# Ternary FFN: the last butterfly of the second Hadamard turn on VectorE and GpSimd; the channel attention as a loop, its first loads, and constant products in the last stage

## The reference, cut to what matters

```python
x = x + channel_attention(layernorm(x), ctx, ctx)      # 32 heads of 16 channels, scores 512 x 512
x = x + ternary_ffn(layernorm(x), w_up, w_down)
x = x + causal_attention(layernorm(x), ctx, ctx)       # 16 heads of 32 channels
x = x + workspace_ffn(layernorm(x), ...)               # two rounds, 16 slots

def hbitlinear(x, w, bits):                            # used twice in ternary_ffn
    xh = fwht(x)                                       # Walsh-Hadamard over the last axis, / sqrt(n)
    xq = act_quant(xh, bits)                           # per token: round(x * 127 / absmax)
    return xq @ weight_quant(w).T                      # weights -1, 0, 1 times a scale

h = hbitlinear(x, w_up, 8)                             # 512 -> 1024
out = hbitlinear(square(relu(h)), w_down, 8)           # 1024 -> 512
```

## Time and profile before

| | us |
|---|---|
| runs (3) | 3765.82, 3773.39, 3771.95; median 3771.95 |
| profiled execution | 3779.81 |
| its span in the profile | 3777.9 |
| busy PE, DVE, ACT, POOL | 3537.5, 2887.7, 2554.2, 1741.6 |

### The profile page before, as it was taken

The page is one execution under the profiler, slowest core; times in us unless marked ns, Lnnn a source line. Parts: engine busy times, 40 slices in busy tenths (PEclk is TensorE's granted clock), DMA queues, the critical chain, the costliest instruction groups (busy, mean ns, idle before and its releaser), DMA issues. The chain is left out here.

```text
span 3777.9 us, 73028 instructions
## 1 busy us (share of the span) xinstructions
PE 3537.5 (94%) x25219; PEld 1778.8 (47%) x25219; DVE 2887.7 (76%) x4445; ACT 2554.2 (68%) x6417; POOL 1741.6 (46%) x2148
## 2 busy tenths in 40 slices
PE   6999999999999999889999979999997999999997
PEld 1222222222222222278788855555554666666664
DVE  7888888888888888768878858888886466574745
ACT  3777777777777777667777758878875454545454
POOL 5444444444444444077666624554553233342524
PEclk9999999999999999989999989999999999999999
DMA  7777677676677777433333313333452022120402
GB/s 123 123 124 124 120 122 123 118 123 121 120 124 124 124 124 138 125 99 124 116 118 115 117 61 101 108 107 103 129 177 86 1 68 68 41 95 4 132 1 79
DMA packets 344317, 392.11 MB, mean 104 GB/s; under 512 B 58640, under 2 KB 223120, under 8 KB 343952
## 3 DMA queue, kind: packets, MB, share of 16 engines
q1 hardware_dynamic: 316464, 352.03, 42.0%
q10 hardware_dynamic: 27488, 35.41, 3.7%
HBM read 200.65 MB, written 84.93 MB: 76 GB/s over the span
## 5 line engine op out<-in xcount | busy, mean ns | idle before, releaser
L385 DVE TENSOR_REDUCE a_neg_max<-a_max_ps 128x2 f32<-128x1024 f32 x1024 | 1209.9, 1220 | 199.6 <-PE a_max_ps L497 189.9
L529 ACT ACTIVATE a_P<-a_ring_ps 128x512 f32<-128x512 f32 x2048 | 1085.4, 603 | 407.7 <-PE a_ring_ps L477 398.5
L497 PE MATMUL a_max_ps<-a_K,a_Q 96*128 96x512 bf16 x2048 | 621.3, 385 | 32.6 <-DMA a_Q<-a_q_split 24.6
L477 PE MATMUL a_ring_ps<-a_Q,a_K 98*128 98x512 bf16 x2048 | 627.6, 384 | 14.4 <-DMA a_Q<-a_max_rows 10.1
L514 PE MATMUL a_pv_ps<-a_P,a_V 128*32 128x512 f32 x4096 | 545.7, 605 | 1.8 <-ACT a_out_sb L534 1.8
L477 PEld LDWEIGHTS a_ring_ps<-a_Q,a_K 98*128 98x128 bf16 x2048 | 157.9, 96 | 681.4 <-ACT a_P L529 497.8
L1334 ACT ACTIVATE c_P<-c_s_ps,c_bias 128x128 f32<-128x128 f32 x1024 | 368.1, 384 | 65.1 <-DVE c_bias L1170 64.8
L324 POOL TENSOR_SCALAR a_var_eps<-a_mean_var 128x1 f32<-128x1 f32 x64 | 12.3, 192 | 765.1 <-DVE a_mean_var L401 765.1
L497 PEld LDWEIGHTS a_max_ps<-a_K,a_Q 96*128 96x128 bf16 x2048 | 188.9, 98 | 220.8 <-DMA a_Q<-a_q_split 24.6
L1165 DVE TENSOR_REDUCE c_neg_max<-c_s_ps 128x4 f32<-128x512 f32 x256 | 175.7, 686 | 81.5 <-PE c_s_ps L1260 75.0
L1334 ACT ACTIVATION_READ_ACCUMULATOR c_P<-c_s_ps,c_bias 128x1 f32 x1024 | 228.4, 223 | 0.0
(11 more groups left out here) (271 smaller groups left out, 7267.7 us busy)
## 6 DMA issues: line engine op xcount, KB each, us to landing
a_K<-a_k_split SPq DMA_DIRECT2D x384, 128.0 KB, 7.1
a_Q<-a_q_split SPq DMA_DIRECT2D x378, 128.0 KB, 4.6
heads_out<-a_out_sb ACTq DMA_DIRECT2D x128, 256.0 KB, 4.6
w_first_in<-in_x_dram SPq DMA_DIRECT2D x112, 256.0 KB, 3.6
w_second_in<-in_ctx_dram SPq DMA_DIRECT2D x64, 256.0 KB, 4.9
w_third_in<-in_ctxT_dram SPq DMA_DIRECT2D x64, 256.0 KB, 5.0
x<-b_x SPq DMA_DIRECT2D x64, 256.0 KB, 2.1
c_x_in<-x SPq DMA_DIRECT2D x64, 256.0 KB, 3.6
```

The lines of the kernel that those rows point to most:

```text
L385: dve.tensor_reduce(neg_max[:, p, 2 * u:2 * u + 2], max_ps[u % 2][:, :, :], AX.X, ALU.max, negate=True).then_inc(max_taken, 1)
L477: pe.matmul(ring(s, use_of(k))[:, :], K[i][:, h, n:n + 128], Q[i][:, h, :], start=True, stop=True).then_inc(scores_filled, 1)
L497: last = pe.matmul(max_ps[u % 2][:, j, :], Q[i][0:KROW, h, m:m + 128], K[i][0:KROW, h, :], start=True, stop=True)
L529: act.activation(P[p][k // NT][:, k % NT, :], ring(s, use_of(k))[:, :], ACT.Exp, scale=SCALE).then_inc(exp_done, 1)
```

## The change

In the channel attention `run_steps` keeps the first and last steps unrolled and runs those between in a loop of six steps a turn: 20 turns on TensorE and ScalarE, 19 on SyncE, GpSimd and VectorE. GpSimd makes the first batch's V two steps earlier, and SyncE issues the parts of batch 1 ahead of the inputs of batch 3.

```diff
-def run_steps(eng, first, last, body):
-
-    for k in range(first, last + 1):
+def run_steps(eng, first, loop_from, loop_to, last, body):
+
+    assert (loop_to - loop_from) % 6 == 0
+    for k in range(first, loop_from):
         body(Step(0, k))
+    with eng.Fori(0, (loop_to - loop_from) // 6) as turn:
+        for k in range(6):
+            body(Step(turn, loop_from + k))
+    for k in range(loop_to, last + 1):
+        body(Step(0, k))
...
+                if s.k == -2:
+                    transfer_parts(s)
+                load_rows(s)
...
+                if s.k != -2:
+                    transfer_parts(s)
+            run_steps(sp, -8, 2, 116, 126, step)
...
+                if s.half(3) == 0 and s.exists(3) and s.k != -3:
+                    split_values(s.batch(3), s.slot(3), s.lap(3))
+                if s.k == -5:
+                    split_values(0, 0, 0)
+            run_steps(pool, -6, 4, 118, 126, step)
...
+            run_steps(dve, -7, 1, 115, 125, step)
...
+            run_steps(pe, -2, 2, 122, 128, step)
...
+            run_steps(act, -1, 4, 124, 129, step)
```

```diff
@@ pool: the order of a step
+                if t.k == 0:
+                    scale_heads(0)
+                if t.exists(5):
+                    b, i = t.batch(5), t.slot(5, 2)
+                    pool.wait_ge(uc_done, b + 1)
+                    at_least(pool, t2_filled, b - 1)
+                    v = uc[:, :].rearrange("p (a o d) -> p a o d", a=2, o=2)
+                    w = u[i][:, 4:IK, :].rearrange("p (a o) d -> p a o d", o=2)
+                    pool.tensor_tensor(w[:, :, 1], v[:, :, 0], v[:, :, 1], ALU.subtract).then_inc(u_low_done, 1)
                 if t.exists(2):
...
                     pool.tensor_tensor(x1[:, j, :], x_in[i][:, :], scaled[:, :], ALU.add).then_inc(x1_done, 1)
+                if t.exists(-1):
+                    scale_heads(t.batch(-1))
+                if t.exists(1):
+                    b, j = t.batch(1), t.slot(1, 8)
+                    pool.wait_ge(moments_done, b + 1)
...
@@ vector
-                    dve.tensor_tensor(u[i][:, h:IK].rearrange("p k d -> p (k d)"), ua[:, 0:I // 2], ua[:, I // 2:I], ALU.subtract).then_inc(u_done, 1)
+                    at_least(dve, u_low_done, b)
+                    dve.tensor_tensor(uc[:, :], ua[:, 0:I // 2], ua[:, I // 2:I], ALU.subtract).then_inc(uc_done, 1)
                 if t.exists(1):
...
+                if t.exists(3):
+                    b, i = t.batch(3), t.slot(3, 2)
+                    dve.wait_ge(uc_done, b + 1)
...
+                    dve.tensor_tensor(w[:, :, 0], v[:, :, 0], v[:, :, 1], ALU.add).then_inc(u_done, 1)
@@ tensor
-                    pe.wait_ge(u_done, b * 2 + 2)
+                    pe.wait_ge(u_done, b * 2 + 1)
                     at_least(pe, rnd2_done, b)
-                    for k in range(0, IK, 2):
+                    for k in range(0, IK // 2, 2):
                         pe.matmul(t2_ps[:, k * 128:(k + 2) * 128], u[i][:, k, :], had[:, 0:256], start=True, stop=False)
...
+                    pe.wait_ge(u_done, b * 2 + 2)
+                    pe.wait_ge(u_low_done, b + 1)
+                    for k in range(IK // 2, IK):
+                        last = pe.matmul(t2_ps[:, k * 128:(k + 1) * 128], u[i][:, k, :], had[:, 0:128], start=True, stop=True)
```

```diff
+def keep_busy(pe, bank, tile, n):
+
+    for _ in range(n):
+        pe.matmul(bank, tile[:, :], tile[:, :].unsqueeze(1).to_broadcast([128, 4, 128]), start=True, stop=True)
...
+                    if f.k == 0:
+                        keep_busy(pe, xb_ps[1][:, :], w.spare, 11)
```

More of the change, by code:

```diff
@@ L247, in load_weights, with load_rows, transfer_parts @@
                 sp.dma_start(w_in[:, c, :].rearrange("p (k n) -> p k n", k=src.shape[1]), src).then_inc(w_loaded[c], 16)
+            def load_rows(s):
+                if s.half(8) == 0 and s.exists(8):
+                    b, i = s.batch(8), s.slot(8)
+                    at_least(held, q_split_done, b - (NB - 1))
+                    at_least(held, k_split_done, b - (NB - 1))
+                    at_least(held, v_done, b - (NB - 1))
+                    sp.dma_start(x_in[i][:, :], by_channel(x[b])).then_inc(x_loaded[i], 16)
+                    sp.dma_start(c_in[i][:, :], by_channel(ctx[b])).then_inc(c_loaded[i], 16)
+                    sp.dma_start(cT_in[i][:, :].rearrange("p (t c) -> p t c", t=NT), ctxT[b].rearrange("(t p) c -> p t c", p=128)).then_inc(cT_loaded[i], 16)
+            def transfer_parts(s):
+                if s.half(4) == 0 and s.exists(4):
+                    b, i = s.batch(4), s.slot(4)
+                    if s.k != -4:
+                        held.wait_ge(q_split_done, b + 1)
+                    held.wait_ge(k_split_done, b + 1)
+                    at_least(held, scores_filled, (b - (NB - 1)) * (2 * SCORES))
+                    if s.k != -4:
+                        for n, part in enumerate((0, 0, 1, 1, 0, 2)):
+                            sp.dma_start(Q[i][n * D:(n + 1) * D, :, :], q_split[:, i, part, :]).then_inc(Q_loaded[i], 16)
+                    for n, part in enumerate((0, 1, 0, 1, 2, 0)):
+                        sp.dma_start(K[i][n * D:(n + 1) * D, :, :], k_split[:, i, part, :]).then_inc(K_loaded[i], 16)
             def step(s):
@@ L361, in step @@
                         pool.wait_ge(preset, 2 + 2 * i)
-                if s.half(3) == 0 and s.exists(3):
-                    b, i = s.batch(3), s.slot(3)
-                    held.wait_ge(cT_loaded[i], s.lap(3) * 16 + 16)
-                    at_least(held, pv_done, (b - (NB - 1)) * (2 * NT))
-                    pool.tensor_scalar(V[i][:, :, :, 0:D], cT_in[i][:, :].rearrange("p (t h d) -> p t h d", t=NT, d=D), 1.0, 0.0,
-                                       ALU.mult, ALU.add).then_inc(v_done, 1)
-            run_steps(pool, -6, 126, step)
+                if s.half(3) == 0 and s.exists(3) and s.k != -3:
[3 more added lines that the diff above has]
+            run_steps(pool, -6, 4, 118, 126, step)
             pool.memset(w_half[:, :], 0.5).then_inc(preset, 1)
@@ new lines, in scale_heads @@
+            def scale_heads(b):
+                i = b % 4
+                pool.wait_ge(o_loaded[i], b // 4 * 16 + 16)
+                pool.wait_ge(r_loaded[i], b // 4 * 16 + 16)
+                at_least(pool, x1_done, b)
+                pool.tensor_tensor(scaled[:, :], o_in[i][:, :], r_in[i][:, :], ALU.mult).then_inc(scaled_done, 1)
+            def step(t):
+                if t.k == 0:
[7 more added lines that the diff above has]
+                    pool.tensor_tensor(w[:, :, 1], v[:, :, 0], v[:, :, 1], ALU.subtract).then_inc(u_low_done, 1)
```

87 lines of the change are left out of this document (43 added, 44 removed).

## The result

The changed kernel takes 3858.85 us (median of 4 runs, 3855.94 to 3864.55) against 3769.44 us for the kernel before (4 runs): a ratio of 1.0239, 95% interval 1.0221 to 1.0257. It is slower by some 89 us; 3847 us was forecast. The profiled execution took 3861.3 us (span 3859.5), 81.6 us of span more than that of before.

The account below looks back on a forecast made before the run. TensorE was taken to bound the attention and ternary FFN; terms 64 - 5 - 4 + 20 = +75 us on the median 3771.95 gave 3847 us, with 3790 to 3900 us for 8 times in 10.

Parts of the forecast that it names:

- the ring: Ternary FFN: inversion, `r_in` load, `scaled`, shift, `z`, relu and VectorE's butterfly wait on each other, 20.6 us per two batches.
- attention, beginning: Start of the attention: batch 1's parts issued 11 us sooner, so TensorE's 4.69 us idle time goes; -5 us.
- workspace FFN: Workspace FFN: products run at full instead of partly half clock, added products lie almost all in TensorE's waits; -4 us.
- attention, loop: Attention's loop: jumps back make engines fetch their lists anew, 1 us at each of 20 turns; +20 us.
- FFN, TensorE: Ternary FFN, second turn: TensorE's products fall from 3.44 to 2.67 us, freeing 0.77 us a batch, which becomes idle time.
- FFN, the new order: Ternary FFN, GpSimd: `scaled` ahead of rstd and shift makes `z` wait for `r_in`; 10.3 us a batch, +64 us.
- that butterfly to the inversion: Ternary FFN, VectorE: from its first butterfly to the inversion, without idle time, 6.28 us.
- FFN, VectorE and GpSimd: Ternary FFN: VectorE's added 256-element sum costs some 0.3 us; GpSimd's added difference is by itself hidden.
- rival with the dear jump: Attention's loop: each jump back costs 3.5 us in place of 1; 3897 us in all, chance 0.17.
- keep the pace: Rival, ternary FFN: `r_in` lands soon enough, TensorE sets the pace and the kernel is faster; 3734 us, chance 0.12.
- softer slack: Rival, ternary FFN: the load lands in about 3.5 us, 9.45 us a batch; 3795 us in all, chance 0.06.
- rival with the free loop: Attention's loop costs nothing; 3827 us in all, the low part of the main case, without a chance of its own.

Follow-up runs that it names:

- beginning alone: The kernel before, unrolled, with only the attention's new beginning (first batch's V sooner on GpSimd, batch 1's parts ahead of the input loads on SyncE): 3759.01 us.
- loop alone: The kernel before with only the channel attention's loop of six half steps a turn, on all five engines: 3749.45 us.
- squares first: The changed kernel with VectorE's inversion at the head of its step, SyncE reordered, and ScalarE's two squares ahead of its second rounding: 3698.72 us.
- early inversion: The changed kernel with VectorE's inversion moved from behind the residual to the head of its step and SyncE's output store behind the row loads: 3728.81 us.
- old order: The changed kernel, split butterfly included, with GpSimd's eps, power and shift ahead of the head product again, as in the kernel before: 3787.24 us.
- loads held back: The kernel before, unrolled, with one more SyncE wait on ScalarE's exponentials ahead of the attention's input loads, from batch 5 on: 3767.77 us.

## Why the prediction was right, and where it was wrong

The time and its sign were right, 12 us off, and the ring that makes the kernel slower is the one forecast. That the total came so near is in part luck: the FFN was put 48 us too low and the loop 38 us too high.

| term | forecast | measured |
|---|---|---|
| FFN: ring against TensorE | +64 | +112 (FFN of after against 626) |
| attention, beginning | -5 | -4 [-8 to -1] (beginning alone) |
| workspace FFN | -4 | -1.6 in the profile, not separable |
| attention, loop | +20 | -18 [-23 to -13] (loop alone) |

*FFN, TensorE.* Right: the part with 256 columns and the four products of 128 columns (eight records) from 1955.06 on are what was counted. Where nothing waits (squares first) the step is 8.37 us, 0.72 under the 9.09 of the loop alone, for 0.77 forecast. In the change as made it became idle time, as said.

*FFN, the new order.* The mechanism is the one forecast, link by link, and its alternation over two batches too. The term was undersized by 48 us. The ring was put at 10.3 us a batch; from the first inversion in this stage to the last it is 11.00 us over the 60 intervals, which is 42 us more. The steps that were mis-sized are "that butterfly to the inversion ... 6.28 us" with "the new sum: 0.3 us" (7.54 us in the mean for 6.58), and "`scaled`: 1.28 us" with "rstd and shift ... 1.20 us" (2.92 for 2.48). The earlier trace rows showed the sums in a phase in which they met nothing and VectorE did not wait for `q`, and the durations were taken for constants. The remainder, some 6 us, is the base: the pace of 9.24 us was read in the profiled execution of before, whose FFN was 7 us over its siblings.

The collision has a plain form in the traces: of VectorE's sum and GpSimd's `scaled` the one that starts second runs only after the first. In the changed kernel 25 of the 72 sums from 1750 to 2150 us overlap a `scaled`. The 13 that start after it all end 0.54 or 0.55 us behind its end, wherever they started, and take 0.78 to 1.76 us. The 12 that start ahead of it take 0.68 or 0.69 us, and there `scaled` takes up to 1.69 us in place of 1.27. The Trainium skill ("GPSIMD Engine Reference", "Specifications") lists the SBUF interfaces of GpSimd as shared with VectorE, with contention for VectorE's instructions with two SBUF inputs. The trace agrees: these sums read two SBUF tiles. The butterflies that read one input from PSUM never meet `scaled` in the changed kernel, but 42 of them do in the one with the early inversion, and none takes over 0.69 us.

*FFN, VectorE and GpSimd.* "By itself this is hidden" was wrong. With the old order the split still costs 54 us of FFN: the difference stands behind the late load and ahead of the sums of z, in a second ring that the prediction did not look for. It needed no new wait on anything slow, since the slow load was already there.

*Attention, the loop.* The step that failed is the jump's price, "I take 1 us, nearer the short end". It rested on "each makes an engine fetch its list anew", and that did not happen: the changed kernel loads no instructions from 157 us, in the second turn, to 1499 us, behind the last turn's branch, where the straight form made 48 and 41 loads from 300 to 1400 us alone. TensorE's branch takes 0.208 us at the median and 0.243 at most, 20 times, no product waits behind it, and the attention is 18 us shorter. The rival with the dear jump is out. The Trainium skill ("Runtime: NRT & Kernel Launch", "Instruction fetch mechanics") ties the stall to a target outside the fetched window; with no load over these turns the targets were inside, so its stall was not tested here. The forecast had also let no row speak for a gain beyond the 12.6 us ahead of L477; the other half lay ahead of L486, a line that was not read.

*Attention, the beginning.* Right: the parts start at 23.64 us, as forecast at 23.5, and the 4.69 us of TensorE are gone (the score product at 45.32 is followed by the next at 46.17).

*Workspace FFN.* The call of L1872 (L1823 before) went from 5.57 to 3.84 us, as forecast:

```profile
3014.28 3.84 PE L1872 MATMUL d_F<-d_wsT,d_wk_sb 128*128 128x128 f32 x32 [0.26 <-ACT d_wsT L2105]
3017.96 3.74 PE L1872 MATMUL d_F<-d_wsT,d_wv_sb 128*128 128x128 f32 x32
```

The granted clock of this stretch is 0.91 for 0.69. But the stage as a whole took 876.5 for 878.1 us, and the kernels without the added products took 875.6 to 878.6. A gain of this part can't be told from the spread, and the products alone weren't tried.

*The rivals.* TensorE does not keep the pace, because the landing is 5.08 us (5.25 in the mean), as argued; with the inversion moved and the squares first, it does. The dear jump and the softer slack are out by the rows above. Of the rival with the free loop the mechanism is true and its 3827 us are not, since the ring took more.

## What to carry to other kernels

Before a slow load is put into a new place of an engine's order, list every closed path that goes through it, those that are hidden today too, and compare each with the pace of the bound engine; the second longest decides what the next edit costs. The cure is often at the other end: here the producer of the load's data, moved 6 us ahead in its engine's order, brought two orders that had been 58 us apart to within 2 us, and only then did the saved TensorE work count. Durations taken from one phase of the engines hold for that phase: when an order is shifted, see what comes to lie beside what.

## What the runs showed of the hardware

The same fp32 sum of two SBUF tiles (128x512) on VectorE took 0.68 us alone, and up to 1.76 us in the changed kernel when it started after GpSimd's product of the same shape: then it ended 0.55 us behind the product. Started ahead of it, the sum kept 0.68 us and the product grew from 1.27 to as much as 1.69 us. With one input in PSUM the sum kept 0.69 us beside the product (early inversion).

The loop over six groups a turn cost less than its straight form. From its second turn on it loaded no instructions, where the straight form had loaded 16 KB for TensorE every 23 us. The branch took 0.208 us on TensorE and 0.050 us on ScalarE at the median, without a visible stop, and the gain of 13 to 25 us came from TensorE's loop alone.

The row maxima landed 0.7 us sooner (5.0 to 4.3 us) with the loads held back, and the time did not change.
